# MoE stage: all sorted rows loaded in four transfers at the start, all results kept in SBUF until stored

## The chip, the cores and the metric

One core of a Trainium2 chip. The metric is the device time of one execution in microseconds, as the median of several runs.

## What is computed

A two-layer network on x of shape (1, 2048, 128), float32: a mixing layer, then attention plus two Mamba scans plus a mixture of experts (MoE). The change touches the MoE alone. Cut to what matters:

```
hn2 = _layernorm(x, ln2_g, ln2_b).reshape(-1, h)
logits = hn2 @ gate_w + gate_b
idx = jnp.argmax(logits, axis=-1)
mid = jax.nn.relu(jnp.einsum('th,ehf->etf', hn2, w1) + b1[:, None, :])
y = jnp.einsum('etf,efh->eth', mid, w2) + b2[:, None, :]
moe = y[idx, jnp.arange(hn2.shape[0])]
return x + moe.reshape(b, s, h)
```

Each of the 2048 tokens goes to one of 8 experts; an expert has w1 (128 x 512) and w2 (512 x 128).

## The kernel before

The program is a row of stages with a barrier between them: layer 0, attention, Mamba in both directions, `moe_prep_stage`, `moe_stage`, and the store of the output.

`moe_prep_stage` normalises the tokens, finds each token's expert, and sorts: every expert gets whole tiles of 128 rows, 23 tiles (`NSLOT`) at most in all. POOL scatters the normalised rows to their sorted places in a DRAM tensor (`x_rows` in the profile, `S.x_dram`), which was filled with zeros before by one transfer (L1372). `S.eid` holds the expert of each tile, `S.wall` all experts' weights in SBUF.

`moe_stage` goes through the 23 tiles. Per tile s:

- SP loads the tile's 128 rows into one of three buffers (`load`, L1520), once TensorE has finished the output of tile s-3 (`y_psum`). After each load it issues `store(s - 2)` (L1524), which waits for ACT's copy of that tile's result. Loads and stores stand in one queue, in the order load(s), store(s-2), load(s+1), store(s-1).
- DVE reads the tile's expert and copies that expert's weights into one of three buffers `cur` (L1577), once TensorE has finished the output of tile s-3.
- TensorE transposes the rows (L1589; the profile shows one record), does the first product as four matmuls (L1611; eight records), a product of a row of ones with the bias b2 (L1594; two records, one row of contraction), and the second product as four matmuls that add to it (L1597; eight records). Its program order is shifted: turn(s+1), first product of s, bias row and second product of s-1.
- ACT scales and shifts the transposed rows (L1548, `xT`), applies bias and relu to the first product (L1565, four activations, `mid`), and copies the result from PSUM to one of two `y` buffers (L1555), which waits for the store of tile s-2 too.

At the end POOL waits for all stores, gathers the rows back into the tokens' order with 16 indirect transfers (L1539), and DVE adds them to the residual (L1581).

PSUM has two banks each for the transposes, the first product and the result.

Of the kernel before, what the change touches and what calls it, by code (L numbers as in the profile page):

```python
# [17 lines left out]
ACT = mybir.ActivationFunctionType  # L18
AX = mybir.AxisListType

P = 128
# [12 lines left out]
NFB = NF // P  # L34
NSLOT = NT + NE - 1
# [30 lines left out]
def natural(dram):  # L66

    return dram.rearrange("o (i p) d -> p (o i) d", p=P)


def layer0_stage(nc, S, dr):

    with ExitStack() as ctx:
        def sb(name, shape, dt=F32):
            return ctx.enter_context(nc.sbuf_tensor(name, shape, dt))
# [27 lines left out]
        kact = sb("l0_kact", [P, T])  # L103
        W = sb("l0_w", [P, 3, P])
        sc = sb("l0_sc", [P, 16])
# [26 lines left out]
        def _(sp):  # L132
            sp.dma_start(S.vec[:, :], dr["vecs"]).then_inc(vec_in, 16)
            for q in range(4):
                sp.dma_start(X[:, 4 * q:4 * q + 4, :], natural(dr["x"])[:, 4 * q:4 * q + 4, :]).then_inc(x_in[q], 16)
            sp.dma_start(W[:, :, :], dr["w_mix"].rearrange("m c d -> c m d")).then_inc(w_in, 16)
            sp.wait_ge(w_in, 16)
# [175 lines left out]
        def _(pe):  # L313
# [10 lines left out]
            def value(c):  # L324
                pe.wait_ge(sq_done, c + 1)
                if c >= 2:
                    pe.wait_ge(val_free, c - 1)
                pe.matmul(banks[4 + c % 2][:, :], W[:, 2, :], kact[:, c * CH:(c + 1) * CH],
                          start=True, stop=True).then_inc(val_done, 1)

            for c in range(NCH):
                if c >= 2:
                    pe.wait_ge(act_done, 2 * (c - 1))
                pe.matmul(banks[2 * (c % 2)][:, :], W[:, 0, :], xr[:, c * CH:(c + 1) * CH],
                          start=True, stop=True).then_inc(proj_done, 1)
                pe.matmul(banks[2 * (c % 2) + 1][:, :], W[:, 1, :], xk[:, c * CH:(c + 1) * CH],
                          start=True, stop=True).then_inc(proj_done, 1)
# [32 lines left out]
def attention_prep_stage(nc, S, dr):  # L370

    with ExitStack() as ctx:
        def sb(name, shape, dt=F32):
            return ctx.enter_context(nc.sbuf_tensor(name, shape, dt))
# [3 lines left out]

        W = sb("ap_w", [P, 3, P])
        bv = sb("ap_bv", [P, P])  # L380
# [1105 lines left out]
def moe_stage(nc, S, dr):  # L1486

    with ExitStack() as ctx:  # L1488
        def sb(n, shape, dt=F32):
            return ctx.enter_context(nc.sbuf_tensor(f"xe_{n}", shape, dt))  # L1490

        def sem(n):
            return S.enter_sem(nc, f"xe_{n}")

        W = 3
        cur = sb("cur", [P, W, WROW])
        x, xT = sb("x", [P, W, P]), sb("xT", [P, 2, P])
        mid, y = sb("mid", [P, 2, NFB, P]), sb("y", [P, 2, P])
        ones = sb("ones", [1, P])
        picked = sem("picked")  # L1500
        moved = sb("moved", [P, NT, P])
        t_bank, m_bank, y_bank = S.banks[0:2], S.banks[2:4], S.banks[4:6]
        loaded = [sem(f"loaded{w}") for w in range(W)]
        stored = [sem("stored0"), sem("stored1")]
        gathered = [sem(f"gathered{c}") for c in range(NCH)]
        turned, xT_ready, mid_psum, mid_ready, y_psum, y_ready = (sem("turned"), sem("xT_r"), sem("mid_psum"), sem("mid_r"),
                                                                  sem("y_psum"), sem("y_r"))
        ones_ready, added = sem("ones_r"), sem("added")
        block = ctx.enter_context(nc.Block())

        def V(n):
            return S.vec[:, VCOL[n]:VCOL[n] + 1]

        @block.sync
        def _(sp):
            def load(s):
                w = s % W
                if s >= W:
                    sp.wait_ge(y_psum, s - W + 1)
                sp.dma_start(x[:, w, :], S.x_dram[P * s:P * (s + 1), :]).then_inc(loaded[w], 16)  # L1520

            def store(s):
                sp.wait_ge(y_ready, s + 1)
                sp.dma_start(S.y_dram[P * s:P * (s + 1), :], y[:, s % 2, :]).then_inc(stored[s % 2], 16)  # L1524

            for s in range(NSLOT):
                load(s)
                if s >= 2:
                    store(s - 2)
            store(NSLOT - 2)  # L1530
            store(NSLOT - 1)

        @block.gpsimd
        def _(pool):
            pool.memset(ones[:, :], 1.0).then_inc(ones_ready, 1)
            pool.wait_ge(stored[0], 16 * ((NSLOT + 1) // 2))
            pool.wait_ge(stored[1], 16 * (NSLOT // 2))
            for i in range(NT):
                pool.indirect_dma_start(moved[:, i, :], None, S.y_dram,  # L1539
                                        bass.IndirectOffsetOnAxis(ap=S.pos[:, i:i + 1], axis=0)).then_inc(gathered[i // TPC], 16)  # L1540

        @block.scalar
        def _(act):
            def turn(s):
                act.wait_ge(turned, s + 1)
                if s >= 2:
                    act.wait_ge(mid_psum, s - 1)
                act.activation(xT[:, s % 2, :], t_bank[s % 2][:, 0:P], ACT.Identity, bias=V("ln2_b"),  # L1548
                               scale=V("ln2_g")).then_inc(xT_ready, 1)

            def out(s):
                act.wait_ge(y_psum, s + 1)
                if s >= 2:
                    act.wait_ge(stored[s % 2], 16 * (s // 2))
                act.activation(y[:, s % 2, :], y_bank[s % 2][:, 0:P], ACT.Copy).then_inc(y_ready, 1)  # L1555

            turn(0)
            for s in range(NSLOT):
                if s + 1 < NSLOT:
                    turn(s + 1)  # L1560
                act.wait_ge(mid_psum, s + 1)
                if s >= 2:
                    act.wait_ge(y_psum, s - 1)
                for f in range(NFB):
                    act.activation(mid[:, s % 2, f, :], m_bank[s % 2][:, P * f:P * (f + 1)], ACT.Relu,  # L1565
                                   bias=cur[:, s % W, NF + f:NF + f + 1]).then_inc(mid_ready, 1)
                if s >= 1:
                    out(s - 1)
            out(NSLOT - 1)

        @block.vector
        def _(dve):
            for s in range(NSLOT):
                e = dve.value_load(S.eid[0:1, s:s + 1], min_val=0, max_val=NE - 1)
                if s >= W:
                    dve.wait_ge(y_psum, s - W + 1)
                dve.tensor_copy(cur[:, s % W, :].unsqueeze(1), S.wall[:, bass.ds(e, 1), :]).then_inc(picked, 1)  # L1577
            for c in range(NCH):
                dve.wait_ge(gathered[c], 16 * TPC)
                r = S.res[:, TPC * c:TPC * (c + 1), :]  # L1580
                dve.tensor_tensor(r, r, moved[:, TPC * c:TPC * (c + 1), :], ALU.add).then_inc(added, 1)  # L1581

        @block.tensor
        def _(pe):
            def turn(s):
                pe.wait_ge(loaded[s % W], 16 * (s // W + 1))
                if s >= 2:
                    pe.wait_ge(xT_ready, s - 1)
                pe.transpose(t_bank[s % 2][:, 0:P], x[:, s % W, :], S.ident[:, :]).then_inc(turned, 1)  # L1589

            def output(s):
                if s >= 2:
                    pe.wait_ge(y_ready, s - 1)
                pe.matmul(y_bank[s % 2][:, 0:P], ones[:, :], cur[0:1, s % W, B2_AT:WROW], start=True, stop=False)  # L1594
                for f in range(NFB):
                    pe.wait_ge(mid_ready, NFB * s + f + 1)
                    mm = pe.matmul(y_bank[s % 2][:, 0:P], mid[:, s % 2, f, :], cur[:, s % W, W2_AT + P * f:W2_AT + P * (f + 1)],  # L1597
                                   start=False, stop=(f == NFB - 1))
                mm.then_inc(y_psum, 1)

            pe.wait_ge(ones_ready, 1)
            turn(0)
            for s in range(NSLOT):
                if s + 1 < NSLOT:
                    turn(s + 1)
                pe.wait_ge(xT_ready, s + 1)
                if s >= 2:
                    pe.wait_ge(mid_ready, NFB * (s - 1))
                pe.wait_ge(picked, s + 1)
                for f in range(NFB):  # L1610
                    mm = pe.matmul(m_bank[s % 2][:, P * f:P * (f + 1)], cur[:, s % W, P * f:P * (f + 1)], xT[:, s % 2, :],  # L1611
                                   start=True, stop=True)
                mm.then_inc(mid_psum, 1)
                if s >= 1:
                    output(s - 1)
            output(NSLOT - 1)
# [94 lines left out]
```

## Time and profile before

| | us |
|---|---|
| median of 3 runs | 1839.95 |
| lowest and highest run | 1839.89, 1840.34 |
| the profiled execution | 1845.69 |
| its span, first to last instruction | 1844.0 |
| mean granted TensorE clock over the span | 0.747 |
| `moe_stage`: first SP issue to POOL's last gather | 1646.79 to 1835.04 |

Times in the rows below are microseconds from the span's start, unless marked ns. PE is TensorE's matmuls, PEld its weight loads, DVE VectorE, ACT ScalarE, POOL GpSimd, SP SyncE, which issues transfers. L12 is line 12 of the kernel. The tiles of `moe_stage` begin with `xe_`. The granted clock is a share of TensorE's full 2.4 GHz; 0.50 is 1.2 GHz. An end that names an engine or a transfer behind "<-" says what released the instruction from an idle time.

### The profile page before, as it was taken

How to read it: one execution, taken by the hardware profiler on the slowest of the kernel's cores; microseconds unless marked ns; L12 is line 12 of the kernel's file. 1: busy time of each engine (PE TensorE's matmuls, PEld its weight loads, DVE VectorE, ACT ScalarE, POOL GpSimd, SP SyncE). 2: the span in 40 equal slices, each digit the busy share in tenths (PEclk: the TensorE clock that was granted, in tenths of full speed). 3: DMA queues.
4: the chain of work that ended last, by engine and by line, in shares of the span. 5: the costliest groups of instructions: out<-in, count | busy, mean ns of one | idle time of the engine just before them, and what ended most of it. 6: DMA issues, size and time to landing. Idle time of an engine off the chain costs nothing. (4 is left out here: it accounts for less than half of the span.)

```text
span 1844.0 us, 17746 instructions
## 1 busy us (share of the span) xinstructions
PE 1148.8 (62%) x5865; PEld 398.3 (22%) x5865; DVE 1260.3 (68%) x1893; ACT 845.7 (46%) x1217; POOL 508.4 (28%) x473
## 2 busy tenths in 40 slices
PE   0341499999999999999873133337513333526662
PEld 0130022222222222222330000004200000425552
DVE  8943899999999999996111599991139999410000
ACT  2220067777777777777625244431524444202220
POOL 1201000000000000000002699980249999130003
PEclk9765599999999999999986555557855555655555
DMA  0012010001001100000003666600176552310001
GB/s 28 0 62 83 24 58 1 1 22 46 10 1 38 39 1 1 1 2 1 3 19 119 125 127 137 137 1 22 63 171 138 124 108 43 110 59 18 17 18 53
DMA packets 64682, 93.51 MB, mean 51 GB/s; under 512 B 8998, under 2 KB 29750, under 8 KB 64590
## 3 DMA queue, kind: packets, MB, share of 16 engines
q1 hardware_dynamic: 63566, 90.27, 19.8%
q0 software_dynamic: 1024, 2.10, 0.4%
q8 instruction: 47, 0.77, 0.2%
q14 instruction: 45, 0.37, 0.1%
HBM read 74.88 MB, written 17.17 MB: 50 GB/s over the span
## 5 line engine op out<-in xcount | busy, mean ns | idle before, releaser
L658 DVE TENSOR_REDUCE at_mpart<-psum 128x1 f32<-128x512 f32 x1024 | 656.5, 685 | 49.3 <-PE psum L719 30.0
L637 ACT ACTIVATE at_probs<-psum 128x1024 f32<-128x1024 f32 x512 | 496.2, 1021 | 272.8 <-PE psum L748 272.6
L761 PE MATMUL psum<-at_probs,at_vg 128*32 128x512 f32 x2048 | 273.6, 606 | 0.4 <-ACT at_probs L637 0.4
L748 PE MATMUL psum<-at_qs,at_ks 75*128 75x512 bf16 x1024 | 269.3, 384 | 1.3 <-ACT at_probs L637 0.2
L719 PE MATMUL psum<-at_ks,at_qs 64*128 64x512 bf16 x512 | 207.9, 406 | 84.9 <-DMA at_km<-k_parts 50.6
L723 PE MATMUL psum<-at_km,at_qm 64*128 64x512 bf16 x512 | 207.9, 406 | 0.0
L613 POOL CAST at_m<-at_mneg 128x16 bf16<-128x16 f32 x16 | 3.1, 197 | 698.2 <-DVE at_mneg L663 698.2
L1225 POOL TENSOR_TENSOR msf_inject<-msf_dus,msf_bs 128x512 f32<-128x512 f32 x128 | 159.7, 1299 | 28.5 <-DMA msf_cs<-m_bc 28.5
L1225 POOL TENSOR_TENSOR msb_inject<-msb_dus,msb_bs 128x512 f32<-128x512 f32 x128 | 158.4, 1265 | 27.0 <-DMA msb_cs<-m_bc 27.0
L1244 PE MATMUL psum<-msf_hc,m_stack 128*32 128x512 f32 x256 | 61.0, 1042 | 161.6 <-DVE msf_hc L1169 152.6
L1244 PE MATMUL psum<-msb_hc,m_stack 128*32 128x512 f32 x256 | 60.1, 1027 | 160.9 <-DVE msb_hc L1169 151.9
L719 PEld LDWEIGHTS psum<-at_ks,at_qs 64*128 64x128 bf16 x512 | 47.7, 93 | 385.0 <-DVE at_mpart L658 331.1
L1577 DVE COPY xe_cur<-x_wall 128x1156 f32 x23 | 17.5, 763 | 159.0 <-PE psum L1597 134.4
L1153 ACT ACTIVATE psum<-msf_dts,m_aneg 128x512 f32<-128x512 f32 x128 | 85.5, 686 | 48.6 <-DVE msf_hp L1196 19.4
L748 PEld LDWEIGHTS psum<-at_qs,at_ks 75*128 75x128 bf16 x1024 | 78.2, 98 | 135.3 <-issue 52.0
L1153 ACT ACTIVATE psum<-msb_dts,m_aneg 128x512 f32<-128x512 f32 x128 | 85.5, 686 | 47.1 <-DVE msb_hp L1196 19.2
L1196 DVE TENSOR_TENSOR_SCAN psum<-psum,msb_last,msb_inject 128x512 f32<-128x512 f32 x66 | 82.5, 1273 | 0.0
L1196 DVE TENSOR_TENSOR_SCAN psum<-psum,msf_last,msf_inject 128x512 f32<-128x512 f32 x66 | 82.5, 1273 | 0.0
L1539 POOL DMA_INDIRECT xe_moved<-x_done,x_pos x16 | 15.7, 981 | 173.3 <-DMA x_done<-xe_y 168.7
L1589 PE MATMUL psum<-ident,xe_x 128*128 128x128 f32 x23 | 10.8, 472 | 83.4 <-DMA xe_x<-x_rows 83.4
L1239 PE MATMUL psum<-m_u,m_diag 128*32 128x512 f32 x128 | 30.3, 1028 | 49.5 <-PEq L62 49.5
L1169 DVE TENSOR_TENSOR msf_hc<-psum,msf_cs 128x512 f32<-128x512 f32 x88 | 58.6, 667 | 0.0
(273 smaller groups left out, 1421.3 us busy)
## 6 DMA issues: line engine op xcount, KB each, us to landing
msf_dts<-m_dt SPq DMA_DIRECT2D x32, 256.0 KB
msf_dus<-m_dtu SPq DMA_DIRECT2D x32, 256.0 KB
msb_dts<-m_dt SPq DMA_DIRECT2D x32, 256.0 KB
msb_dus<-m_dtu SPq DMA_DIRECT2D x32, 256.0 KB
at_qs<-q_parts SPq DMA_DIRECT2D x48, 96.0 KB
at_ks<-k_parts SPq DMA_DIRECT2D x48, 96.0 KB
msf_bs<-m_bc SPq DMA_DIRECT2D x16, 256.0 KB
msf_cs<-m_bc SPq DMA_DIRECT2D x16, 256.0 KB
```

The source lines that it names most:

```text
L637: act.activation(probs[:, u % 2, p, :], s_pair[p], ACT.Exp, scale=float(HD) ** -0.5).then_inc(probs_ready, 1)
L658: dve.reduce_max(mpart[:, s % 2, 2 * jp + b, i, kc:kc + 1], ring[x % 3], AX.X).then_inc(ring_free, 1)
L719: pe.matmul(ring[x % 3], S.qs[0:HALF, buf, q], S.ks[0:HALF, buf, k], start=True, stop=True)\
L723: pe.matmul(ring[y % 3], S.qm[64:64 + HALF, buf, q], S.km[64:64 + HALF, buf, k], start=True, stop=True)\
L748: mm = pe.matmul(s_banks[p][b], S.ks[0:DM, g % 2, j * T + kt * P:j * T + (kt + 1) * P], S.qs[0:DM, g % 2, j * T + c * CH:j * T + (c + 1) * ...
L761: mm = pe.matmul(o_bank[VW * j:VW * (j + 1), :], vg[:, g % 2, kt, j, :], probs[:, u % 2, j // 2, CH * (j % 2):CH * (j % 2 + 1)], start=(kt ...
L1153: act.activation(decay[k % ND], dts[:, i % 2, j, :], ACT.Exp, scale=S.aneg[:, n:n + 1]).then_inc(decay_ready, 1)
L1169: dve.tensor_tensor(hc[:, r % 2, j, :], hv[by_dve[k] % NH2], cs[:, c % 2, q, :], ALU.mult).then_inc(dve_weighed, 1)
L1196: dve.tensor_tensor_scan(h, decay[k % ND], inject[:, k % NI, :], before if c else 0.0, ALU.mult, ALU.add).then_inc(scanned, 1)
L1225: pool.tensor_tensor(inject[:, k % NI, :], dus[:, i % 2, j, :], bs[:, c % 2, q, :], ALU.mult).then_inc(injected, 1)
L1239: pe.matmul(y_bank[i % 2][GC * j:GC * (j + 1), :], S.diag[:, b, GC * j:GC * (j + 1)], S.u[:, b, cols(c)], start=True, stop=False, tile_pos ...
L1244: mm = pe.matmul(y_bank[i % 2][GC * j:GC * (j + 1), :], S.stack[:, :], hc[:, r % 2, j, :], start=False, stop=(q == NQ - 1), tile_position= ...
```

## The change

`x` grows from 3 tile buffers to 23 and `y` from 2 to 23. SP issues four loads at the start, of 6, 6, 6 and 5 tiles, and then the 23 stores in order. TensorE's transpose of tile s waits for the part that holds it. All stores count on one semaphore, ACT no longer waits for a store, and POOL waits for the one count.

```
-        x, xT = sb("x", [P, W, P]), sb("xT", [P, 2, P])
-        mid, y = sb("mid", [P, 2, NFB, P]), sb("y", [P, 2, P])
+        NX = 4
+        XT = -(-NSLOT // NX)
+        x, xT = sb("x", [P, NSLOT, P]), sb("xT", [P, 2, P])
+        mid, y = sb("mid", [P, 2, NFB, P]), sb("y", [P, NSLOT, P])
...
         def _(sp):
-            def load(s):
-                w = s % W
-                if s >= W:
-                    sp.wait_ge(y_psum, s - W + 1)
-                sp.dma_start(x[:, w, :], S.x_dram[P * s:P * (s + 1), :]).then_inc(loaded[w], 16)
-
             def store(s):
                 sp.wait_ge(y_ready, s + 1)
-                sp.dma_start(S.y_dram[P * s:P * (s + 1), :], y[:, s % 2, :]).then_inc(stored[s % 2], 16)
+                sp.dma_start(S.y_dram[P * s:P * (s + 1), :], y[:, s, :]).then_inc(stored, 16)
+
+            def rows(n):
+                part = slice(XT * n, min(XT * (n + 1), NSLOT))
+                sp.dma_start(x[:, part, :], S.x_dram.rearrange("(s p) d -> p s d", p=P)[:, part, :]).then_inc(x_in[n], 16)
+
+            for n in range(NX):
+                rows(n)
             for s in range(NSLOT):
-                load(s)
-                if s >= 2:
-                    store(s - 2)
-            store(NSLOT - 2)
-            store(NSLOT - 1)
+                store(s)
...
         def _(pool):
             pool.memset(ones[:, :], 1.0).then_inc(ones_ready, 1)
-            pool.wait_ge(stored[0], 16 * ((NSLOT + 1) // 2))
-            pool.wait_ge(stored[1], 16 * (NSLOT // 2))
+            pool.wait_ge(stored, 16 * NSLOT)
...
             def out(s):
                 act.wait_ge(y_psum, s + 1)
-                if s >= 2:
-                    act.wait_ge(stored[s % 2], 16 * (s // 2))
-                act.activation(y[:, s % 2, :], y_bank[s % 2][:, 0:P], ACT.Copy).then_inc(y_ready, 1)
+                act.activation(y[:, s, :], y_bank[s % 2][:, 0:P], ACT.Copy).then_inc(y_ready, 1)
...
             def turn(s):
-                pe.wait_ge(loaded[s % W], 16 * (s // W + 1))
+                pe.wait_ge(x_in[s // XT], 16)
                 if s >= 2:
                     pe.wait_ge(xT_ready, s - 1)
-                pe.transpose(t_bank[s % 2][:, 0:P], x[:, s % W, :], S.ident[:, :]).then_inc(turned, 1)
+                pe.transpose(t_bank[s % 2][:, 0:P], x[:, s, :], S.ident[:, :]).then_inc(turned, 1)
```

## Rows read from the trace of the kernel before

**Rows 1.** The page's second part: granted clock in 40 equal slices, in tenths

```profile
PEclk9765599999999999999986555557855555655555
```

**Rows 2.** Chain that ended last, 1725 to 1733: start, duration, what

```profile
1723.89 1.88 DMA xe_x<-x_rows
...
1725.81 0.48 PE psum L1589
...
1730.75 0.29 ACT xe_y L1555
...
1731.06 0.32 SPq L1524
...
1731.42 1.97 DMA xe_x<-x_rows
```

**Rows 3.** Groups of instructions, 1640 to 1844: busy, mean ns, idle before, releaser

```profile
L1565 ACT ACTIVATE xe_mid<-psum,xe_cur 128x128 f32<-128x128 f32 x92 | 26.2, 368 | 28.4 <-PE psum L1611 28.4
...
L1589 PE MATMUL psum<-ident,xe_x 128*128 128x128 f32 x23 | 10.8, 472 | 83.4 <-DMA xe_x<-x_rows 83.4
L1548 ACT ACTIVATE xe_xT<-psum,vec 128x128 f32<-128x128 f32 x23 | 10.5, 458 | 98.5 <-PE psum L1589 98.5
L1555 ACT ACTIVATE xe_y<-psum 128x128 f32<-128x128 f32 x23 | 6.4, 277 | 36.1 <-PE psum L1597 36.1
```

**Rows 4.** Chain that ended last, 1802 to 1844

```profile
1803.72 0.72 PE psum L1594 x2
...
1806.45 1.71 PE psum L1611 x8
1808.16 0.72 PE psum L1594 x2
...
1813.95 1.51 DMA x_done<-xe_y
```

**Rows 5.** Stretches: length, PE, PEld, DVE, ACT, POOL busy, granted clock, DMA share, GB/s

```profile
1654.00:1655.00 1.00, 1.00 (x9) 0.96 (x8) 0.00 (x0) 0.83 (x4) 0.00 (x0) 1.00 0.00 0
...
1656.00:1657.00 1.00, 0.00 (x0) 0.00 (x0) 0.06 (x1) 0.00 (x0) 0.00 (x0) 0.85 0.27 77
...
1803.00:1806.00 3.00, 3.00 (x13) 2.55 (x13) 0.00 (x0) 1.14 (x4) 0.00 (x0) 0.50 0.01 3
...
1809.00:1812.00 3.00, 3.00 (x12) 2.55 (x13) 0.00 (x0) 0.61 (x3) 0.00 (x0) 0.50 0.00 0
```

**Rows 6.** Instructions in order of time, 1646 to 1656

```profile
1646.79 1.29 SPq L1520 DMA_DIRECT2D xe_x<-x_rows  x3
...
1648.88 0.82 PE L1589 MATMUL psum<-ident,xe_x 128*128 128x128 f32 x2 [30.31 <-DMA xe_x<-x_rows]
...
1649.88 2.08 PE L1611 MATMUL psum<-xe_xT,xe_cur 128*128 128x128 f32 x8 [0.17 <-ACT xe_xT L1548]
...
1651.75 0.42 PE L1589 MATMUL psum<-ident,xe_x 128*128 128x128 f32 x1
...
1651.96 1.69 PE L1611 MATMUL psum<-xe_xT,xe_cur 128*128 128x128 f32 x8
...
1653.58 0.48 PE L1594 MATMUL psum<-xe_cur,xe_ones 1*128 1x128 f32 x2
...
1654.00 1.16 PE L1597 MATMUL psum<-xe_cur,xe_mid 128*128 128x128 f32 x8
```

**Rows 7.** A stretch of the attention's output projection (L834): PE, PEld, granted clock

```profile
916.00:918.00 2.00, 2.00 (x19) 2.00 (x19) 1.00 0.00 0
```

**Rows 8.** TensorE's instructions in order of time, 1650 to 1662

```profile
1657.73 0.48 PE L1589 MATMUL psum<-ident,xe_x 128*128 128x128 f32 x1 [2.57 <-DMA xe_x<-x_rows]
```

**Rows 9.** Instructions in order of time, 0 to 9: layer 0's load and its reader

```profile
1.24 2.07 SPq L135 DMA_DIRECT2D l_x<-in_x  x4
...
4.40 1.64 DVE L216 BATCH_NORM_STATS2 l_st<-l_x 128x6 f32<-128x128 f32 x8 [1.37 <-DMA l_x<-in_x]
```

**Rows 10.** Transfers by line: count, KB each, us from issue to landing

```profile
x_rows<-xp_zeros SPq DMA_DIRECT2D x1, 1472.0 KB, 8.3
```

More of the change, by code:

```diff
@@ L1502, in moe_stage @@
         t_bank, m_bank, y_bank = S.banks[0:2], S.banks[2:4], S.banks[4:6]
-        loaded = [sem(f"loaded{w}") for w in range(W)]
-        stored = [sem("stored0"), sem("stored1")]
+        x_in = [sem(f"x_in{n}") for n in range(NX)]
+        stored = sem("stored")
         gathered = [sem(f"gathered{c}") for c in range(NCH)]
```

## Prediction

> **What bounds the kernel now.** I began with the page: in the last five of its 40 slices, from 1614 us on, the granted clock reads 5 tenths [rows 1]. The change touches only the expert stage, so the next view was the chain of waits that ended last, cut to one tile of that stage. One tile is a closed loop: the transfer of sorted rows (1.88 us), TensorE's four groups from 1725.81 to 1730.73 (transpose, eight matmul records of the first product, two of the bias row, eight of the second product; 4.92), ACT's copy of the result (0.29), SP's issue of the store (0.32), and the next transfer [rows 2]. With the gaps that is 7.53 us, from 1723.89 to 1731.42. The odd link is the last: SP issues store(s-2) only after ACT has written it, and the load of tile s+1 is queued behind that store (L1524 before L1520 in SP's order). TensorE therefore asks for rows that were requested only when it had become idle. The waits of the stage say the same: the transpose's group idled 83.4 us before its records, all of it for this transfer [rows 3]. ACT has 26.2 + 10.5 + 6.4 = 43.1 us of work for 23 tiles, 1.9 us each [rows 3]. So the stage is bound by a round trip, not by an engine.
>
> **What TensorE needs per tile if nothing is late.** The end of the stage shows it: the last tiles have no load to wait for, and in the chain two bias rows begin at 1803.72 and 1808.16 [rows 4]. Between them lie a bias row, a second product and a first product: 4.44 us at a granted clock of 0.50 [rows 4, 5]. A transpose in the middle of a stream adds 0.21 us (1651.75 to 1651.96) [rows 6]. At the 1.2 GHz level a tile is thus 4.65 us.
>
> At the 2.4 GHz level: the attention output's f32 128x128 records, granted 1.00, came 19 in 2.00 us, 0.11 each [rows 7]; eight are 0.90, and the transpose is one more, 0.11. The second product of tile 0 took 1.16 us for its eight in a stretch granted 1.00 [rows 5, 6]; that includes the drain of the last record, under which the next group begins, so it lies between 0.90 and 1.16 and I take 0.96. The bias row took 0.42 (1653.58 to 1654.00) [rows 6]. For the first product, with the hand-over to the bias row, 0.99: at the low level the tail's 4.44 less 0.72 is 3.72 for two products, 1.86 each, of which eight records are 1.71 [rows 4], so 0.15 is hand-over, and I take 0.09 of it. Sum 0.11 + 0.99 + 0.42 + 0.96 = 2.48 us.
>
> **Which clock, as the trace shows it.** Before it rose, TensorE did first product, transpose, first product without a break, from 1649.88; in 1654 to 1655 the granted clock was 1.00 [rows 5, 6]. In 1656 to 1657 it was down to 0.85 on its way to 0.50: the engine was idle from 1655.16 to 1657.73, waiting for the transfer of tile 3 [rows 5, 8]. In the steady loop every tile has such a pause and the clock stays at 0.50. But the tail speaks against an easy answer: from 1803 to 1812 TensorE was busy without a pause and still had 0.50 [rows 5]. The difference I see is the bias row, a one-row product that breaks the stream every 4.44 us. In the changed kernel the opening is the same as before (two transposes, then product, transpose, product), which is what preceded the rise, and after it nothing stops the engine, so I take it that the clock rises at about the same place and is kept. If it misses there, the steady stream still has second product, transpose and first product in one run, much as the product, transpose and product that preceded the rise; each tile of delay costs 4.65 - 2.48 = 2.2 us. I add 1.5 us for that, and keep 0 and 6.6 (three tiles) as ends.
> The Trainium skill (TensorE: Matmul & The Clock Gate, Part 1) says that the throttled state is the default and that activity releases it. By that rule alone the tail should have risen, and it did not; on the changed stream it would give the same sum as mine.
>
> **The change, part by part.**
> 1. The per-tile load and its wait on y_psum go. Between the first bias rows (1653.58) and the end of the last second product (1813.6, the last store's 1813.95 less ACT's copy of 0.3) the kernel now takes 160.0 us [rows 4, 6]. Without late rows: 20 tiles of 2.48 with a transpose, one without (2.37), one with a bias row and a second product only (0.42 + 0.96 = 1.38), and the last bias row and product (0.42 + 1.16 = 1.58): 49.6 + 5.3 = 54.9 us. Gain 105.1 us.
> 2. Four transfers of 384, 384, 384 and 320 KB go out at the start in place of three of 64 KB. The first rows are later. Now: issue 1646.79, transpose 1648.88, 2.1 us [rows 6]. The nearest row is layer 0's load, four transfers of 256 KB in the same arrangement: first issued at 1.24, its reader began at 4.40, 3.2 us [rows 9]. One transfer of 1472 KB landed in 8.3 us [rows 10]; on the line between the two, the 128 KB more are 0.5 us. 3.7 us, that is 1.6 late. Low end 0 (the transfer is as quick as now); high end, if all four share the engines evenly, those 8.3 us, 6.2 late. I take 1.6, by the closer size. Parts two to four land by about 1655, by the same 8.3 us; tile 6 is turned some 15 us after the first.
> The Trainium skill (DMA: Bandwidth & Descriptors, Bandwidth) lists 0.95 us of transfer for 64 KB and 6.15 for 1 MB; an estimate on the line between gives 384 KB 1.8 us more than 64 KB. By it the sum would be 0.2 us longer.
> 3. SP: the four issues are about 0.5 us each, as layer 0's four took 2.07 [rows 9], and over by 1649, six us before the first store is ready. Then only stores stand in its queue; nobody waits on one but POOL at the end. Cost 0.
> 4. ACT's wait on stored goes. It cost nothing: the copies begin when TensorE ends (36.1 us, all TensorE) [rows 3].
> 5. POOL waits for one count instead of two, at the same event. The tail from 1813.6 (copy, store of 1.51 us, 16 gathers, last add) stays [rows 4].
> 6. Next in line: ACT. Its 1.9 us of work per tile must fit in 2.48 with three hand-overs. It does as I lay it out: four mid activations (1.14 in all) while TensorE does bias row and second product, the copy (0.28) when that ends, then the xT activation (0.46), and some 0.3 us free before the next four. 0.05 us a tile for what I can't see: 1 us. DVE's copy of a tile's weights starts when a buffer frees, two tiles ahead: hidden.
> Sum: 105.1 - 1.6 - 1.5 - 1.0 = 101 us. The profiled run took 1845.69 us around its 1844.0 span; the median of the runs is 1839.95, 5.7 lower, and the gain is carried over whole: **1840 us less 101, 1739 us**.
>
> **Rivals.**
> A. The low clock stays, as in the tail. 20 x 4.65 + 4.44, 2.7 for bias row and second product and 2.7 for the last pair = 102.9 us in place of 160.0; with 1.6 for the load the gain is 55.5: 1784.5 us. For it: the busy tail at 0.50. Against it: the same opening did rise. 0.11.
> B. The clock comes and goes, or ACT's hand-overs do not fit and a tile takes 3.3 to 3.5 us (half the tiles at 4.65, half at 2.48 gives 3.57): 22 tiles x 0.9 = 20 us more: 1759 us. For it: only 0.3 us are free on ACT. 0.08.
> C. Slower: the chain that held tiles at 7.5 us turns out to be TensorE to ACT and back, in series (transpose, xT, product, mid, product, copy), and the transfer was hidden anyway. 4.92 on TensorE [rows 2] and 0.46 + 1.14 + 0.28 on ACT [rows 3] = 6.8 us plus hand-overs of 0.1 to 0.3 comes to 7.6, times 21.5 that is 163 in place of 160, and the load's 6.2 us come on top: 1849 us. It decides from a tile of 7.4 us on (160.0 less 1.6, over 21.5). The tail, at 4.44 without any wait, speaks against it. 0.01.
> D. The change does not do what it says, tile loads or stores still throttling: nothing in the new order of SP can; within 0.2%, 0.01.
>
> **The numbers.** Forecast 0.79, A 0.11, B 0.08, C 0.01, D 0.01. A measurement of this kernel can tell about 0.2% (3.7 us) from no change. The forecast's own range is 1733 (no delay for load or clock, nothing unseen, second product at 0.90: 1.6 + 1.5 + 1.0 + 1.3 less) to 1749 (load 4.6 and clock 5.1 worse); with B inside it is 1732 to 1761, leaving out A, C and D, 13 in 100, and the ends. Faster 0.98, same 0.01, slower 0.01.
>
> **What would show it.** Right: no idle before the transposes in the stage, bias rows 2.5 us apart, granted clock 1.00 from about 1655 to the end of the stage, the first transpose near 1650.5, and POOL's first gather near 1714. Wrong in the clock: rows 4.65 apart at 0.50. Wrong in ACT: idle of TensorE put down to xT or mid. Wrong in the load: a first transpose near 1655.

## The result, and the profile after

| | before | after |
|---|---|---|
| median, us | 1839.9 | 1738.5 (1735.7 to 1742.4, 4 runs) |
| the profiled execution, us | 1845.7 | 1739.2 |
| its span, us | 1844.0 | 1737.2 |
| first load's issue to the end of the last product, us | 166.8 | 66.3 |

The ratio is 0.9455, with a 95% interval of 0.9432 to 0.9479. The last row of the table is read from [rows 4, 6] before and from the rows below after (1706.50 less 1640.22): 100.5 us less. The spans differ by 106.8; the other 6 us lie ahead of the stage. Its first issue came at 1646.79 before and at 1640.22 after, and in the kernels below, none of which changes anything ahead of it, it lies anywhere from 1639.3 to 1645.9. That is how far executions differ, and no effect of the change.

The opening of the stage in the changed kernel, instructions in order of time (start, duration, engine, line, operation, names, count, idle time before and what ended it). It answers to [rows 6]:

```profile
1640.22 2.59 SPq L1524 DMA_DIRECT2D xe_x<-x_rows  x4
...
1643.93 0.66 PE L1584 MATMUL psum<-ident,xe_x 128*128 128x128 f32 x2 [31.96 <-DMA xe_x<-x_rows]
...
1648.85 0.79 PE L1589 MATMUL psum<-xe_cur,xe_ones 1*128 1x128 f32 x2
...
1653.44 0.48 PE L1589 MATMUL psum<-xe_cur,xe_ones 1*128 1x128 f32 x2
...
1655.94 0.48 PE L1589 MATMUL psum<-xe_cur,xe_ones 1*128 1x128 f32 x2
...
1656.36 1.16 PE L1592 MATMUL psum<-xe_cur,xe_mid 128*128 128x128 f32 x8
...
1657.35 0.27 PE L1584 MATMUL psum<-ident,xe_x 128*128 128x128 f32 x1
```

The first transpose starts 3.71 us after the first issue. The first two bias rows are 4.59 us apart, the next two 2.50. Stretches of the same kernel, with the columns of [rows 5]:

```profile
1643.00:1650.00 7.00, 5.73 (x23) 4.92 (x24) 0.54 (x1) 3.34 (x11) 0.00 (x0) 0.50 0.62 161
1650.00:1653.00 3.00, 3.00 (x16) 3.00 (x16) 0.76 (x1) 0.77 (x3) 0.00 (x0) 0.50 0.05 14
1653.00:1655.00 2.00, 2.00 (x15) 1.71 (x15) 0.00 (x0) 1.14 (x4) 0.00 (x0) 0.92 0.07 20
1655.00:1665.00 10.00, 10.00 (x79) 9.04 (x78) 3.05 (x4) 7.08 (x24) 0.00 (x0) 1.00 0.09 26
...
1685.00:1705.00 20.00, 20.00 (x153) 17.95 (x151) 5.33 (x7) 13.81 (x47) 0.00 (x0) 1.00 0.10 28
```

After a wait of 0.34 us for ACT in the opening, TensorE is busy through the whole loop, at 0.50 for its first nine us and at 1.00 after that. The chain that ended last (start, duration, what) has no transfer and no ACT in a tile any more; it answers to [rows 2]:

```profile
1655.01 0.11 PE psum L1584
1655.12 0.89 PE psum L1606 x8
1656.01 0.41 PE psum L1589 x2
1656.42 1.09 PE psum L1592 x8
1657.51 0.11 PE psum L1584
...
1705.40 1.10 PE psum L1592 x8
```

And the groups of the stage, which answer to [rows 3]: the transposes' only idle time is the one ahead of the first (83.4 us became 32.0, and of those 83.4 the wait before the first transpose was 30.3 [rows 6]).

```profile
L1560 ACT ACTIVATE xe_mid<-psum,xe_cur 128x128 f32<-128x128 f32 x92 | 26.3, 368 | 11.0 <-PE psum L1606 11.0
...
L1584 PE MATMUL psum<-ident,xe_x 128*128 128x128 f32 x23 | 6.7, 300 | 32.0 <-DMA xe_x<-x_rows 32.0
L1550 ACT ACTIVATE xe_y<-psum 128x128 f32<-128x128 f32 x23 | 6.4, 278 | 10.3 <-PE psum L1592 10.3
```

### The profile page after: what moved, and what is told of

The parts are those of the page before. It is cut to its first block and busy times, and to the rows that moved or that the text cites. A ratio compares the mean times of both kernels' runs of the same rounds, so it can differ in the third digit from the quotient of the medians.

```text
span 1737.2 us, 17705 instructions
## 1 busy us (share of the span) xinstructions
PE 1094.2 (63%) x5865; PEld 354.7 (20%) x5865; DVE 1259.0 (72%) x1893; ACT 843.5 (49%) x1217; POOL 510.9 (29%) x473
## 3 DMA queue, kind: packets, MB, share of 16 engines
q0 software_dynamic: 1024, 2.10, 0.4%
## 5 line engine op out<-in xcount | busy, mean ns | idle before, releaser
L1244 PE MATMUL psum<-msf_hc,m_stack 128*32 128x512 f32 x256 | 60.2, 1029 | 161.9 <-DVE msf_hc L1169 152.1
L1153 ACT ACTIVATE psum<-msb_dts,m_aneg 128x512 f32<-128x512 f32 x128 | 85.5, 686 | 47.2 <-DVE msb_hp L1196 19.2
L1169 DVE TENSOR_TENSOR msb_hc<-psum,msb_cs 128x512 f32<-128x512 f32 x88 | 58.8, 669 | 0.0
L1142 ACT ACTIVATE msf_last<-psum 128x1 f32<-128x1 f32 x66 | 11.3, 171 | 88.9 <-DVE msf_hc L1169 88.9
```

What stands on the lines that cost most here:

```text
L1153: act.activation(decay[k % ND], dts[:, i % 2, j, :], ACT.Exp, scale=S.aneg[:, n:n + 1]).then_inc(decay_ready, 1)
L1169: dve.tensor_tensor(hc[:, r % 2, j, :], hv[by_dve[k] % NH2], cs[:, c % 2, q, :], ALU.mult).then_inc(dve_weighed, 1)
L1244: mm = pe.matmul(y_bank[i % 2][GC * j:GC * (j + 1), :], S.stack[:, :], hc[:, r % 2, j, :], start=False, stop=(q == NQ - 1), tile_position= ...
```

## The experiments

Ratios are to the kernel before, run beside each. "Loop" is the time from the first transpose to the end of the last product in the profiled execution: 164.7 us before, 62.6 in the changed kernel.

### Which half of the change does it

The loads alone, with two y buffers and the store's wait:

```
-        mid, y = sb("mid", [P, 2, NFB, P]), sb("y", [P, NSLOT, P])
+        mid, y = sb("mid", [P, 2, NFB, P]), sb("y", [P, 2, P])
...
                 act.wait_ge(y_psum, s + 1)
+                if s >= 2:
+                    act.wait_ge(stored[s % 2], 16 * (s // 2))
```

> The changed kernel with its four loads, but two y buffers and ACT's wait on the store of tile s-2 again. My theory: the whole gain is in the loads; a store lands 1.9 us after its issue, two tiles of 2.5 us later the buffer is long free, so this equals the changed kernel: 1738 us (1735 to 1742), bias rows 2.5 us apart. Rival: the kept results carry part of it, since tiles are now three times faster and ACT meets the store's wait: ACT idle put down to x_done, 0.5 us or more a tile, 1750 us or more.

Measured: 1742.8 us, ratio 0.9484 (0.9458 to 0.9511), loop 62.6 us. The median is 0.8 us above the range I gave and 4 above the changed kernel's. The intervals of the ratios overlap, though, and the loop is the same. The view of the waits has no wait of ACT for a store:

```profile
ACT xe_mid L1563 <- PE psum L1609: 11.2, 23, 1.8
ACT xe_y L1553 <- PE psum L1595: 10.2, 23, 1.6
```

(engine and line, what it waited for, us in total, times, longest.)

The kept results alone, loads as before:

```
-        mid, y = sb("mid", [P, 2, NFB, P]), sb("y", [P, 2, P])
+        mid, y = sb("mid", [P, 2, NFB, P]), sb("y", [P, NSLOT, P])
...
                 act.wait_ge(y_psum, s + 1)
-                if s >= 2:
-                    act.wait_ge(stored[s % 2], 16 * (s // 2))
```

> The kernel before with 23 y buffers and no store wait on ACT; loads as before, three buffers, queued behind the stores. My theory: the round trip stays whole, 7.5 us a tile at a granted clock of 0.50, 1840 us (1836 to 1842). Rival: ACT's copy was held by the store's wait somewhere; then up to 0.3 us a tile, 1833 us.

Measured: 1838.5 us, ratio 1.0015 (0.9996 to 1.0033), loop 164.3. Keeping the results is worth nothing that can be measured here; the gain comes from the loads.

### Is it the large transfers, or the distance

The kernel before with six x buffers, each load still 64 KB:

```
-        x, xT = sb("x", [P, W, P]), sb("xT", [P, 2, P])
+        XW = 6
+        x, xT = sb("x", [P, XW, P]), sb("xT", [P, 2, P])
...
             for s in range(NSLOT):
                 load(s)
-                if s >= 2:
-                    store(s - 2)
-            store(NSLOT - 2)
-            store(NSLOT - 1)
+                if s >= XW - 1:
+                    store(s - XW + 1)
+            for s in range(NSLOT - XW + 1, NSLOT):
+                store(s)
```

> The kernel before with six x buffers in place of three, loads still 64 KB each, issued three tiles earlier and ahead of the store of five tiles before; three y buffers' worth of nothing else changed (two y buffers). My theory: only the distance between request and use mattered, not the large transfers: 2.5 us a tile at 1.00 from a few tiles in, and the first rows 1.3 us earlier than with 384 KB, so 1737 us (1733 to 1741). Rival: with two y buffers and stores queued behind loads the loop closes again through the store, ACT idle behind x_done, 3 us a tile or more, 1750 us or more.

Measured: 1734.8 us, ratio 0.9441 (0.9417 to 0.9464), loop 60.2. Loads are still issued behind stores, one pair per tile, but each is early. Its instructions in order of time:

```profile
1639.85 2.71 SPq L1521 DMA_DIRECT2D xe_x<-x_rows  x6
1641.87 0.73 PE L1590 MATMUL psum<-ident,xe_x 128*128 128x128 f32 x2 [30.23 <-DMA xe_x<-x_rows]
...
1651.50 0.48 PE L1595 MATMUL psum<-xe_cur,xe_ones 1*128 1x128 f32 x2
...
1653.42 0.32 SPq L1525 DMA_DIRECT2D x_done<-xe_y  x1
1653.78 0.43 SPq L1521 DMA_DIRECT2D xe_x<-x_rows  x1
1654.01 0.48 PE L1595 MATMUL psum<-xe_cur,xe_ones 1*128 1x128 f32 x2
```

The tile takes 2.51 us as in the changed kernel, and the first transpose starts 2.0 us after the first issue instead of 3.7. So all of the gain comes from the distance between request and use. The transfers' size has a small price at the start, which the next run looks at alone.

What had kept the distance short is two waits that end nearly together, and no run parts them. With three buffers the load of tile s+1 must wait until TensorE has finished the output of tile s-2, whatever stands ahead of it in the queue. The store ahead of it adds ACT's copy and its own issue, some 0.6 us (0.29 and 0.32 in [rows 2]). The pause before a transpose is about 2.6 us (2.57 in [rows 8]). By these numbers a change of the order alone would have left most of the pause. The prediction's "odd link", the load queued behind the store, is therefore the smaller part of it, and the rule of three buffers the larger. This is worked out from rows and not tested.

The changed kernel with its four transfers cut as 1, 2, 6 and 14 tiles:

```
-        NX = 4
-        XT = -(-NSLOT // NX)
+        PARTS = [0, 1, 3, 9, NSLOT]
+        NX = len(PARTS) - 1
...
```

> The changed kernel with its four transfers cut as 1, 2, 6 and 14 tiles. My theory: the first transpose waits for its own transfer; it begins 1.9 to 2.2 us after the first issue in place of 3.7, and the stage is 1.5 us shorter: 1737 us. TensorE must not wait at tile 1, 3 or 9 (issues are 0.5 us apart, and tile 9 is turned 25 us later). Rival: all four share the engines, so the first part is no earlier: 1738.5 us.

Measured: 1735.6 us, ratio 0.9454 (0.9421 to 0.9487); the first transpose began 1.9 us after the first issue. In the trace the start is 1.8 us shorter, as expected. The loop is shorter too, 60.3 us, which I had not expected: the granted clock rose 4.4 us after the first transpose, not 9.4 as in the changed kernel (its stretch):

```profile
1647.00:1650.00 3.00, 3.00 (x24) 2.64 (x22) 0.76 (x1) 2.06 (x8) 0.00 (x0) 1.00 0.10 25
```

In the ratio no difference from the changed kernel can be told, so both are what one trace shows, and the times neither confirm nor deny them.

### How much is the clock, how much the wait

The kernel before with six matmuls thrown away where TensorE waits for rows:

```
+            def fill():
+                for _ in range(6):
+                    pe.matmul(S.banks[6][:, 0:P], S.ident[:, :], S.ident[:, :], start=True, stop=True)
...
                 if s >= 1:
                     output(s - 1)
+                    if s + 2 < NSLOT:
+                        fill()
```

> The kernel before, with six matmuls of the identity into an unused PSUM bank after each second product, where TensorE waits for the rows; they are work that is thrown away. It leaves the round trip and takes away the idle time. If idle time is what holds the granted clock at 0.50, the clock goes to 1.00 in the stage and TensorE's 4.92 us of the loop shrink by 2.2 to 2.4: a tile takes 5.2 us, 22 tiles, 1790 us (1785 to 1797). Rival: the clock stays at 0.50 as in the tail, and the fillers (6 x 0.43 = 2.6 us) just fit the wait: 1840 us, or a little above. This splits the 101 us into clock and wait.

Measured: 1794.8 us, ratio 0.9765 (0.9720 to 0.9811), loop 118.5. The chain of one tile, to be held against [rows 2]:

```profile
1679.20 1.84 DMA xe_x<-x_rows
...
1681.09 0.33 PE psum L1589
1681.42 0.90 PE psum L1615 x8
1682.32 0.41 PE psum L1598 x2
1682.74 1.10 PE psum L1601 x8
...
1683.86 0.29 ACT xe_y L1555
...
1684.16 0.32 SPq L1524
...
1684.53 2.04 DMA xe_x<-x_rows
```

The round trip is whole, transfer and all, but TensorE's share is 2.75 us where it was 4.92, and 12 more records of discarded work in each tile made the kernel 2.3% faster. The granted clock was 0.91 to 1.00 in stretches of 20 us from 1655 to 1755. So of the 102.1 us by which the change shortens the loop, 46.2 are the clock (164.7 to 118.5) and 55.9 the wait (118.5 to 62.6), if counted in this order.

### Why the busy tail kept the low clock

The prediction had left this as the puzzle: TensorE busy from 1803 to 1812 and still at 0.50 [rows 5]. Its suspect was the bias row, a product over one row. In the kernel before, that product is now taken over 128 rows, the first ones and the rest zeros: same result, same columns.

```
-        ones = sb("ones", [1, P])
+        ones = sb("ones", [P, P])
...
-            pool.memset(ones[:, :], 1.0).then_inc(ones_ready, 1)
+            pool.memset(ones[:, :], 0.0).then_inc(zeroed, 1)
+            pool.wait_ge(zeroed, 1)
+            pool.memset(ones[0:1, :], 1.0).then_inc(ones_ready, 1)
...
-                pe.matmul(y_bank[s % 2][:, 0:P], ones[:, :], cur[0:1, s % W, B2_AT:WROW], start=True, stop=False)
+                pe.matmul(y_bank[s % 2][:, 0:P], ones[:, :], cur[:, s % W, B2_AT:WROW], start=True, stop=False)
```

> The kernel before with the bias row's product over 128 rows in place of one: ones is a 128x128 matrix whose first row is 1 and the rest 0, so the result and the columns streamed stay the same, and only the share of the array that works changes. My theory: the one-row product is what kept the busy tail (and the steady loop) at a granted clock of 0.50; with full rows the clock rises above 0.50 in parts of the stage, in the tail at the latest, and the time falls by 3 to 20 us: 1820 to 1835. Rival: the one-row product counts like any other and the pause alone decides; then the steady loop stays at 0.50, within 2 us of the kernel before.

Measured: 1811.8 us, ratio 0.9861 (0.9824 to 0.9898), loop 143.8; 22 us below the kernel before beside it, more than I expected. Not all of it is the clock. Where the clock stays at 0.50, a tile takes 7.07 us (transposes at 1766.48 and 1773.55) instead of some 7.5, because the bias product itself is shorter: 0.42 us (1768.46 to 1768.88) instead of 0.72. That makes some 10 us in 23 tiles; the rest is the clock. It comes and goes, with the pause of every tile still there (its stretches):

```profile
1650.00:1660.00 10.00, 4.76 (x27) 4.38 (x26) 1.52 (x2) 2.79 (x11) 0.00 (x0) 0.80 0.10 26
...
1720.00:1730.00 10.00, 7.14 (x33) 6.55 (x31) 0.77 (x2) 3.13 (x11) 0.00 (x0) 0.50 0.05 13
...
1780.00:1790.00 10.00, 7.91 (x47) 7.72 (x47) 0.00 (x0) 3.55 (x12) 0.00 (x0) 0.72 0.08 23
```

The last stretch is the tail, and now it rises, 5 us after the last pause (0.50 until 1785.5, 1.00 from 1786). The opposite test is on the changed kernel: one more one-row product per tile, result thrown away, no wait added:

```
             def turn(s):
                 pe.wait_ge(x_in[s // XT], 16)
                 if s >= 2:
                     pe.wait_ge(xT_ready, s - 1)
+                    pe.matmul(S.banks[6][:, 0:P], ones[:, :], ones[:, :], start=True, stop=True)
```

> The changed kernel with one more one-row product (ones by ones, into an unused PSUM bank, thrown away) ahead of every transpose from tile 2 on: second product, one-row, transpose, first product, bias row. No wait is added and TensorE never idles. If one-row products hold the clock down, it stays at 0.50 for much of the stage: 4.65 + 0.8 = 5.5 us a tile, 23 tiles, 1795 to 1805 us if always, and this is the price the changed kernel escaped. Rival: a busy TensorE rises whatever it does: 2.5 + 0.5 = 3.0 us a tile, 1748 to 1752 us.

Measured: 1801.3 us, ratio 0.9795 (0.9773 to 0.9817), loop 124.8. Its stretches:

```profile
1660.00:1680.00 20.00, 20.00 (x76) 16.73 (x75) 2.70 (x4) 7.04 (x23) 0.00 (x0) 0.50 0.03 10
...
1740.00:1760.00 20.00, 20.00 (x77) 16.68 (x76) 3.05 (x4) 6.35 (x20) 0.00 (x0) 0.50 0.05 14
```

TensorE is busy for all of 20.00 us of each stretch and is granted 0.50 throughout. A tile takes 5.56 us (second products at 1699.61 and 1705.17), of which the extra product is 0.91 over the 4.65 of [rows 4, 6]. One small product per tile, 0.9 us of work, cost 62 us.

The end of the same trace says something else. The last extra product begins at 1762.77. What follows it is the stream of the tail of the kernel before, group for group, with one one-row product per tile. There the clock rises:

```profile
1764.00:1770.00 6.00, 6.00 (x26) 5.36 (x25) 0.00 (x0) 1.87 (x6) 0.00 (x0) 0.50 0.07 22
1770.00:1771.00 1.00, 1.00 (x5) 0.76 (x5) 0.00 (x0) 0.85 (x4) 0.00 (x0) 0.67 0.00 0
1771.00:1773.00 2.00, 2.00 (x16) 1.76 (x16) 0.00 (x0) 0.56 (x3) 0.00 (x0) 1.00 0.00 0
```

That is some 7 us after the last extra product. The tail of the kernel before kept 0.50 for the whole of its 12.1 us (1801.54 to 1813.6), and so did that of the kernel with the kept results alone.

The extra product again, with both small products over 128 rows. The bias product's operands and the filling of `ones` are changed as in the kernel before with full rows:

```
-        ones = sb("ones", [1, P])
+        ones = sb("ones", [P, P])
...
-            pool.memset(ones[:, :], 1.0).then_inc(ones_ready, 1)
+            pool.memset(ones[:, :], 0.0).then_inc(zeroed, 1)
+            pool.wait_ge(zeroed, 1)
+            pool.memset(ones[0:1, :], 1.0).then_inc(ones_ready, 1)
...
+                    pe.matmul(S.banks[6][:, 0:P], ones[:, :], ones[:, :], start=True, stop=True)
```

> The same extra product ahead of every transpose as in the run before, and the bias product, both over 128 rows in place of one (first row ones, the rest zeros). Same number of products, same columns, same waits; only the rows of the array that work differ. If rows decide the clock, it rises in the first ten us of the stage and stays at 1.00: 2.10 us a tile (full-row bias) plus 0.22 for the extra product, 2.33, so 22 x 0.22 = 5 us above the full-row version, 1733 to 1737 us. Rival: what held the clock at 0.50 was the number or the shortness of the products; then it stays at 0.50 and the time is 1790 us or more.

Measured: 1733.6 us, ratio 0.9431 (0.9396 to 0.9466), loop 56.8; granted clock:

```profile
1650.00:1660.00 10.00, 10.00 (x92) 10.00 (x91) 3.68 (x5) 7.97 (x26) 0.00 (x0) 1.00 0.10 28
1660.00:1680.00 20.00, 20.00 (x182) 20.00 (x180) 6.19 (x9) 15.63 (x53) 0.00 (x0) 1.00 0.11 32
```

The two kernels differ in the rows of two products and in nothing else that TensorE is given to stream, and they are 68 us apart. So one-row products can hold a busy TensorE at the low level. Through which of their traits is not shown: each also takes longer than a full-row one (0.72 against 0.43 us at the low level) and leaves the weight loads idle for 0.2 us.

For the tail of the kernel before, the bias row is a part of the answer and not all of it. With full rows the tail rose, but with one-row products the same stream rose in one trace and not in two others. In the changed kernel, with one of them per tile, the rise took over 9 us, not much less than the 12.1 us of the tail, so the tail may have ended before a rise was due. What sets the moment stays open.

### What the bias row costs at the high level

The changed kernel with the full-row bias product and no extra one, `ones` filled as above:

```
-        ones = sb("ones", [1, P])
+        ones = sb("ones", [P, P])
...
-                pe.matmul(y_bank[s % 2][:, 0:P], ones[:, :], cur[0:1, s % W, B2_AT:WROW], start=True, stop=False)
+                pe.matmul(y_bank[s % 2][:, 0:P], ones[:, :], cur[:, s % W, B2_AT:WROW], start=True, stop=False)
```

> The changed kernel with the same full-row bias product. My theory: the first rise comes no later than in the changed kernel, in the profile before the second bias row, so the loop from the first transpose to the last product is 60 to 62 us in place of 62.6; time 1736 to 1739. Rival: the rise comes at the same place, whatever the rows: 62.6 us. A slower result would mean that a product over 128 rows costs TensorE more than one over one row (0.42 us now at the high level).

Measured: 1728.6 us, ratio 0.9423 (0.9388 to 0.9458), loop 52.2. I expected a loop 1 to 2 us shorter by an earlier rise, and it is 10.3 us shorter. The reason is in its instructions in order of time:

```profile
1659.33 0.27 PE L1586 MATMUL psum<-ident,xe_x 128*128 128x128 f32 x1
...
1659.43 1.06 PE L1608 MATMUL psum<-xe_xT,xe_cur 128*128 128x128 f32 x8
...
1660.22 0.30 PEld L1591 LDWEIGHTS psum<-xe_cur,xe_ones 128*128 128x128 f32 x2
1660.33 0.39 PE L1591 MATMUL psum<-xe_cur,xe_ones 128*128 128x128 f32 x2
...
1660.55 1.06 PE L1594 MATMUL psum<-xe_cur,xe_mid 128*128 128x128 f32 x8
...
1661.44 0.27 PE L1586 MATMUL psum<-ident,xe_x 128*128 128x128 f32 x1
```

A tile is 2.11 us (1659.33 to 1661.44) where the changed kernel has 2.50; over 22 tiles that is 8.6 of the loop's 10.3. The rest is an earlier rise of the clock, 6.1 us after the first transpose instead of 9.4. The bias product takes 0.22 us (1660.33 to 1660.55) instead of 0.42 (1655.94 to 1656.36), the first product hands over to it after 0.90 us (1659.43 to 1660.33) instead of 0.99 (1654.95 to 1655.94), and the second product to the next transpose after 0.89 instead of 0.99. In this stream a bias product over 128 rows is cheaper than one over a single row. The weight loads show where the time goes: here the one of the bias product begins 0.11 us ahead of its matmul, while in the changed kernel the two begin together:

```profile
1655.94 0.29 PEld L1589 LDWEIGHTS psum<-xe_cur,xe_ones 1*128 1x128 f32 x2
```

### A version that beats both

No bias product at all: DVE adds the bias while it takes the result out of PSUM, in place of ACT's copy.

```
+            def out(s):
+                dve.wait_ge(y_psum, s + 1)
+                dve.tensor_tensor(y[:, s, :], y_bank[s % 2][:, 0:P], cur[:, s % W, B2_AT:WROW], ALU.add).then_inc(y_ready, 1)
...
                 if s >= W:
-                    dve.wait_ge(y_psum, s - W + 1)
+                    out(s - W)
+                    dve.wait_ge(y_ready, s - W + 1)
...
-                pe.matmul(y_bank[s % 2][:, 0:P], ones[:, :], cur[0:1, s % W, B2_AT:WROW], start=True, stop=False)
```

> A version meant to beat both: no bias product on TensorE; DVE, which works 0.76 us of 2.5 per tile, adds the bias while it takes the result out of PSUM (one 128x128 add in place of ACT's copy), and the weight copy of a tile stands behind that add. My theory: TensorE is now the bound, so its 0.42 us per tile goes: 2.1 us a tile, 23 x 0.42 = 9.7 us less, and the clock rises a little earlier: 1727 to 1730 us. Rival: DVE's add and its 0.76 us copy in a row after each product, or ACT's 1.6 us, become the round trip, and a tile stays at 2.5 us or more: 1738 us or above.

Measured: 1724.3 us, ratio 0.9382 (0.9346 to 0.9418), loop 47.2. A tile is 1.90 us: the 0.42 of the bias product went, and so did 0.18 of the hand-overs around it, which I had not counted, so the time lies 3 us below my range. The clock also rose earlier than in the changed kernel, 6.3 us after the first transpose. With the transfers cut as 1, 2, 6 and 14 tiles as well:

> The bias on DVE and the transfers cut as 1, 2, 6 and 14 tiles, both together. The two act at different places (1.9 us a tile in the loop, first transpose 1.9 us after the issue in place of 3.5), so they add: 47.2 us of loop as with DVE alone, or 1 to 3 less if the rise comes earlier, and 1.6 us at the start; 1.5 to 3 us below the version with the bias on DVE, so 1720 to 1724 us. Rival: small transfers leave TensorE waiting at tile 3 or 9 now that a tile takes 1.9 us: no gain, 1724 or above.

Measured: 1721.5 us, ratio 0.9357 (0.9337 to 0.9377), loop 46.2, the first transpose 2.0 us after the issue. This is the fastest kernel of the study, 18 us below the changed one, which ran beside it (1739.4). Its interval overlaps that of the version above. Its instructions in order of time:

```profile
1660.18 0.27 PE L1584 MATMUL psum<-ident,xe_x 128*128 128x128 f32 x1
...
1660.38 0.29 DVE L1563 TENSOR_TENSOR xe_y<-psum,xe_cur 128x128 f32<-128x128 f32 x1 [0.33 <-PE psum L1591]
...
1660.81 0.76 DVE L1570 COPY xe_cur<-x_wall 128x1156 f32 x1
...
1662.07 0.27 PE L1584 MATMUL psum<-ident,xe_x 128*128 128x128 f32 x1
```

DVE's add (0.29 us) and copy (0.76) fit into the 1.89 us between two transposes.

### The changed kernel again

> The changed kernel once more, unchanged, beside the others on one chip, to see how far a run of the same program moves: 1738.5 us within 3 us, the loop from first transpose to last product 60 to 65 us by where the clock rises.

Measured: 1739.4 us (1735.5 to 1740.5), ratio 0.9457 (0.9438 to 0.9476), loop 62.8. Differences of 2 us between medians are not to be read.

## Why the prediction was right, point by point

The forecast was 1739 us, its terms 105.1 - 1.6 - 1.5 - 1.0 = 101; the median moved by 101.4. That the two agree within half a us is better than the terms were: some were too small, one was not needed, and they cancelled.

- **The round trip as the bound**: right. Without it no transpose but the first waits for a transfer, and six early buffers do the same as 23. The kept results cost and bring nothing (parts 3 to 5 at zero). The reading of the loop laid too much on the store ahead of the load, as said with the six buffers; the forecast did not hang on it, since the change takes both waits away.
- **A tile at the high level, 2.48 us**: measured 2.50. The second product with its drain left out was put at 0.96 and took 0.99 (1656.36 to the transpose at 1657.35), the bias row 0.42 as read.
- **The load, 3.7 us to the first transpose**: 3.71, by interpolation between two sizes. The hit to the hundredth is luck: in six other executions that start with the same four transfers it was 3.5 to 3.9. The high end, transfers that share the engines evenly (8.3 us), did not happen: the first part was in use after 3.71. From the table of the Trainium skill (DMA: Bandwidth & Descriptors, Bandwidth) the prediction estimated 1.8 us between 64 and 384 KB, and so a sum 0.2 longer. Done again with 1 MB as 1024 KB that estimate is 1.7. The traces show 1.6 here, and 1.4 to 1.8 in the six others, so they do not decide between the two.
- **The clock**: the level was right, the place was not. I took the opening to be followed by the rise, as in the kernel before; the first bias row (1648.85) and the product after it ran at 0.50, and the rise came one tile later, 9 us after the first transpose. From the first bias row to the last product the kernel took 57.6 us (1648.85 to 1706.50), against 54.9 + 1.5 + 1.0 = 57.4. The first tile took 4.59 instead of 2.48, so the clock cost 2.1 where 1.5 was allowed, tiles of 2.50 made another 0.5, and of ACT's allowance of 1.0 nothing was used. The opening ahead of the first bias row was 0.2 us longer than before (4.92 against 4.70).
- **"The same opening did rise"**: the reason given was too weak, and the traces side by side show it. In all seven profiled executions whose first transfer was 64 KB, the kernel before among them, the rise came 4.2 to 4.6 us after the first transpose. In the three with a first transfer of 384 KB and one one-row product per tile (the changed kernel twice, and the loads alone) it came after 9.4 to 9.9, and in the three with that transfer and no one-row product after 5.9 to 6.3. The groups on TensorE up to the first bias row are nearly the same in all but the kernel with a full-row extra product. The later rise lengthens the loop from some 60.2 to 62.7 us. Why the size of the first transfer goes with it is not shown.
- **ACT as the next in line**: it did fit, without a wait of TensorE after the opening. Even at 1.90 us a tile it does, since the copy is gone from it.
- **Rival A, the low clock**: did not happen, but it was a close neighbour. One more one-row product in each tile makes it come true, at 1801 us, near A's 1784.5 with 21 extra products of 0.9 us added (1803). The prediction set it aside because the same opening had risen before; the runs give another reason: the stream has one one-row product per tile and not two. **Rival B**: seen in the kernel before with full rows (0.50 to 0.82 in stretches of 10 us), not in the changed one, where the clock never fell before the work ended. **Rivals C and D** did not occur.

The Trainium skill (TensorE: Matmul & The Clock Gate, Part 1) says that activity releases the throttle. The changed kernel agrees with it, at 1.00 from the second bias row on. The kernel with two one-row products per tile does not, if activity only means that TensorE is busy: it was, for over 100 us without a pause (1650 to 1760 and on), and stayed at 0.50.

## What to carry to other kernels

When an engine waits in each pass for a transfer that was requested only after its own last result, ask for it a few passes earlier; a few small buffers do as well as one for everything. Read the granted clock beside the wait: here the pause cost 56 us by itself and another 46 by holding TensorE at 1.2 GHz, counted in that order. And look at what TensorE streams, not only whether it is busy: here a bias added by a one-row matmul was paid three times, in its own time, in slower hand-overs and in a later rise of the clock, and an idle VectorE added it for nothing.

## What the runs showed of the hardware that I had not expected

- A TensorE that is never idle can stay at 0.50 for 100 us, if two of its eleven matmuls per tile work on one row; with those two over 128 rows it was at 1.00 (1801.3 against 1733.6 us). At the end of the same trace, where one of the two is gone from the stream, it rose within 8 us.
- The clock rose 4.2 to 4.6 us after the first transpose in the seven executions that began with a transfer of 64 KB, and after 9.4 to 9.9 us in three executions that began with 384 KB and had the same products.
- Discarded matmuls in a pause made a kernel faster (1794.8 against 1837.7 us).
- A one-row product between full ones took 0.42 us at the high level, a full one 0.22; the one-row one also cost 0.09 us more at the hand-over from the product before it and 0.10 at that to the next transpose.
- Of four transfers of some 384 KB issued together, the first was usable 3.71 us after its issue (3.5 to 3.9 in six other executions), and one of 64 KB 1.9 to 2.1 us after its own.
